# Two-layer transformer kernel: experts for all tokens against experts for the tokens that chose them

## The chip, the cores and the metric

The kernel runs on one core of a Trainium2 chip. The metric is the device time of one execution in microseconds (us). A core has TensorE (PE), VectorE (DVE), ScalarE (ACT), GpSimd (POOL) and SyncE (SP); each runs its own instruction list in order, and they wait for one another with semaphores. DMA transfers are issued here from SP and, after the change, from POOL too. PE writes into eight PSUM banks, which DVE and ACT read.

## What is computed

Two transformer layers on `x` of 4 batches x 512 tokens x 256 numbers. The first layer (softmax attention and a plain linear layer) and the second layer's linear attention with 16 heads stay as they are. The change is in the last part, the second layer's feed-forward with 8 experts of width 176, of which each token uses two, and one shared expert of the same width:

```python
logits = jnp.einsum('th,eh->te', x, gate_w)
scores = jax.nn.softmax(logits, axis=-1)
topk_w, topk_idx = lax.top_k(scores, 2)
topk_w = topk_w / (topk_w.sum(-1, keepdims=True) + 1e-20)
cw = jnp.zeros((T, 8)).at[jnp.arange(T)[:, None], topk_idx].add(topk_w)
def body(acc, ew):
    w1e, w2e, cwe = ew                  # 256 x 352 and 176 x 256
    g, u = jnp.split(x @ w1e, 2, axis=-1)
    return (acc + cwe[:, None] * (jax.nn.silu(g) * u @ w2e), None)
moe, _ = lax.scan(body, jnp.zeros_like(x), (w1, w2, cw.T))
shared = (silu(x @ sw1.T) * (x @ sw2.T)) @ sw3.T
```

The layer's output is `x + gb * (moe + shared)`. All of it is float32.

## The kernel before, in words

Three stages run one after the other, with a barrier between them: `front_stage`, `attention1_stage` and `experts_stage`. `x` (16 tiles of 128 tokens), the normalized tokens `h_parts` and the attention output `yacc` stay in SBUF.

A float32 product is made of three matmuls: both operands are split into a high part (a copy to the format fp32r by ACT) and a low part (a subtraction by DVE or POOL), and `TERMS` names the pairs high-high, high-low and low-high that are summed in PSUM.

**Attention stage.** The 16 heads go in 8 pairs (`over_pairs`: the first, a loop over six, the last; SP's own loop loads for the next pair). While one pair is worked on, SP loads the next pair's weights (L1152, 1 MB into `wraw`), which ACT splits at the end of the pair (L1295) and POOL completes (L1503). In the last pair `LateNorm` already normalizes batch 0 for the experts. At the stage's end SP loads the first weight tiles of the experts.

**Experts stage.** The hidden units of the 8 experts (8 x 176 = 1408, 11 tiles of 128) and of the shared expert (2 tiles) form 13 tiles. For each of 4 batches and each of 13 tiles PE makes gate and up (L1635: two times six matmuls of 512 tokens), ACT takes silu (L1772), DVE multiplies (L1886, L1893), ACT and DVE split the product (L1748, L1842), and PE multiplies it with the down weights into the output (L1647: twelve matmuls of 256 columns), one tile behind. Routing is a factor: a small matmul (L1718) spreads each token's eight weights over the hidden units, zero for six of the experts, and DVE multiplies with it (L1890). So each token passes through all experts. The routing weights of the next batch (logits L1659, the two largest scores, L1794 to L1821) and its norm (POOL's L968, L980, L983, L996, L998, ACT's L974, PE's L956, L1011) are made in between, at set tiles of the batch before (`ahead`). The weights arrive in the first batch: SP loads a tile (L1620), ACT copies the high part (L1733), POOL subtracts the low part (L1924). At each batch's end DVE applies the layer's gate (L1850), POOL adds to `x` (L1930), SP stores (L1623, and L1627 for the last batch).

The order on every queue is written out by hand; there is no planner.

## Time and profile before

| | us |
|---|---|
| median of three executions | 1311.54 (1310.83 to 1311.84) |
| the profiled execution, its own time | 1312.52 |
| its span, first to last instruction | 1310.8 |
| front stage | 0 to 311.7 |
| attention stage | 311.7 to 1050.4 |
| experts stage | 1050.4 to 1310.8 |

The profile is of one execution. Busy time leaves out register, semaphore and DMA-issuing instructions. Matmuls overlap, so the sum of their durations is more than the time they take together. PEclk is the clock granted to TensorE as a share of 2.4 GHz. "Idle before, releaser" is how long an engine stood before a group and which instruction ended it.

### The profile page before, as it was taken

The page shows a single profiled execution, that of the slowest core. Times are in us where ns is not written, and L with a number is a line of the kernel's source. Part 1 is how long each engine was busy: PE and PEld are TensorE (multiplying, and loading weights), DVE is VectorE, ACT ScalarE, POOL GpSimd, SP SyncE. Part 2 cuts the span into 40 slices and gives each one's busy share as a digit, 9 for nine tenths or more (in the row PEclk, how much of TensorE's full clock was granted, in tenths as well). Part 3 has the DMA queues.
Part 4 walks back from the last instruction along what each step waited for, and adds up shares of the span by engine and source line. Part 5 has one row for each costly group of instructions (what it writes and reads, how often), then busy time and mean ns, then how long its engine had stood idle before and what let it go on. Part 6 is the DMA issues. An engine that isn't in the chain of part 4 may idle for free. (4 is left out here: it accounts for less than half of the span.)

```text
span 1310.8 us, 21088 instructions
## 1 busy us (share of the span) xinstructions
PE 1174.9 (90%) x7620; PEld 992.9 (76%) x7620; DVE 917.2 (70%) x1619; ACT 727.7 (56%) x1315; POOL 350.7 (27%) x305
## 2 busy tenths in 40 slices
PE   5878787743999999999999999999999879999998
PEld 4545565533988988988989889889888758888886
DVE  4578888614777778787777777787788656565544
ACT  4568676623766665656566666656565434333322
POOL 6275453423112121121121121211213145202000
PEclk8689888956999999999999999999999889999999
DMA  7100001001001001000010010010000022000000
GB/s 279 50 29 5 17 3 49 1 1 56 9 1 49 10 9 40 8 16 32 8 48 8 2 46 8 8 40 8 17 25 1 0 84 61 18 0 17 1 17 17
DMA packets 16451, 35.94 MB, mean 27 GB/s; under 512 B 3330, under 2 KB 5634, under 8 KB 15363
## 3 DMA queue, kind: packets, MB, share of 16 engines
q1 hardware_dynamic: 16386, 35.09, 8.3%
q8 instruction: 40, 0.66, 0.2%
q14 instruction: 25, 0.20, 0.1%
HBM read 26.69 MB, written 6.29 MB: 25 GB/s over the span
## 5 line engine op out<-in xcount | busy, mean ns | idle before, releaser
L1194 PE MATMUL attn_psum<-all_h_parts,attn_wp 128*128 128x512 f32 x1152 | 304.2, 400 | 8.4 <-POOL attn_wp L1503 8.4
L1194 PEld LDWEIGHTS attn_psum<-all_h_parts,attn_wp 128*128 128x128 f32 x1152 | 213.8, 191 | 50.4 <-POOL attn_wp L1503 8.8
L1331 ACT CAST attn_pp<-attn_p 128x512 fp32r<-128x512 f32 (+3 forms) x256 | 117.2, 458 | 219.1 <-DVE attn_p L1412 219.0
L1393 DVE TENSOR_TENSOR attn_pp<-attn_p,attn_pp 128x512 fp32r<-128x512 f32 (+3 forms) x256 | 192.5, 752 | 2.3 <-ACT attn_pp L1331 2.3
L1513 POOL TENSOR_TENSOR all_gate<-all_gate,attn_sq 128x512 f32<-128x512 f32 x64 | 91.4, 1428 | 330.4 <-ACT attn_sq L1342 330.4
L1261 PE MATMUL attn_psum<-attn_qkp 128*128 128x512 f32 (+3 forms) x768 | 165.6, 325 | 4.1 <-DVE attn_qkp L1393 4.1
L1220 PE MATMUL attn_psum<-attn_pp,attn_vp 128*128 128x512 f32 (+3 forms) x768 | 163.0, 322 | 0.0
L1635 PE MATMUL experts_psum<-all_h_parts,experts_wf 128*128 128x512 f32 x624 | 156.4, 398 | 0.0
L1220 PEld LDWEIGHTS attn_psum<-attn_pp,attn_vp 128*128 128x128 f32 x768 | 130.0, 190 | 19.6
L1261 PEld LDWEIGHTS attn_psum<-attn_qkp 128*128 128x128 f32 x768 | 125.6, 190 | 12.9 <-issue 4.6
L1635 PEld LDWEIGHTS experts_psum<-all_h_parts,experts_wf 128*128 128x128 f32 x624 | 114.2, 189 | 24.5 <-DVE experts_wf L1874 0.5
L1393 DVE TENSOR_TENSOR attn_yp<-attn_y,attn_yp 128x512 fp32r<-128x512 f32 x64 | 67.3, 1052 | 92.3 <-ACT attn_yp L1339 92.3
L1412 DVE TENSOR_TENSOR attn_p<-attn_psum,attn_mask 128x512 f32<-128x512 f32 (+3 forms) x256 | 123.7, 483 | 5.3 <-PE attn_psum L1261 3.8
L757 DVE TENSOR_REDUCE front_top<-front_psum 128x2 f32<-128x256 f32 (+3 forms) x128 | 100.6, 816 | 34.2 <-PE front_psum L463 34.0
L1204 PE MATMUL attn_psum<-attn_wop,attn_yp 128*128 128x256 f32 x768 | 105.0, 288 | 17.2 <-DVE attn_yp L1393 17.2
L1204 PEld LDWEIGHTS attn_psum<-attn_wop,attn_yp 128*128 128x128 f32 x768 | 98.6, 197 | 19.0 <-DVE attn_yp L1393 19.0
L1189 PE MATMUL attn_psum<-attn_wp,all_h_parts 128*128 128x256 f32 x768 | 102.3, 282 | 1.1
L606 ACT ACTIVATE front_probs<-front_psum 128x1024 f16<-128x1024 f32 (+3 forms) x128 | 83.7, 705 | 33.5 <-PE front_psum L470 33.3
L1393 DVE TENSOR_TENSOR attn_qkp<-attn_qk,attn_qkp 128x512 fp32r<-128x512 f32 x128 | 88.8, 694 | 18.1 <-ACT attn_qkp L1306 18.1
L1189 PEld LDWEIGHTS attn_psum<-attn_wp,all_h_parts 128*128 128x128 f32 x768 | 95.0, 188 | 3.5 <-ACT attn_qk L1303 3.5
L1647 PE MATMUL experts_psum<-experts_wf,experts_hidp 128*128 128x256 f32 x624 | 91.2, 295 | 6.2 <-DVE experts_hidp L1842 6.2
L1647 PEld LDWEIGHTS experts_psum<-experts_wf,experts_hidp 128*128 128x128 f32 x624 | 82.4, 192 | 9.1 <-DVE experts_hidp L1842 7.2
(241 smaller groups left out, 1743.4 us busy)
## 6 DMA issues: line engine op xcount, KB each, us to landing
all_wraw<-in_w1p SPq DMA_DIRECT2D x8, 1024.0 KB, 4.8
all_wraw<-in_wf SPq DMA_DIRECT2D x13, 384.0 KB, 3.2
attn_mask<-decay_masks SPq DMA_DIRECT2D x16, 256.0 KB, 2.6
all_x<-in_x SPq DMA_DIRECT2D x4, 512.0 KB, 10.9
decay_masks<-all_wraw SPq DMA_DIRECT2D x8, 256.0 KB, 5.8
decay_masks<-all_yacc SPq DMA_DIRECT2D x8, 256.0 KB, 8.4
front_kt<-front_kall SPq DMA_DIRECT2D x64, 32.0 KB, 1.9
attn_woraw<-in_wout SPq DMA_DIRECT2D x8, 256.0 KB, 2.6
```

The lines of the kernel that those rows point to most:

```text
L757: nc.vector.tensor_reduce(top[:, tt, h:h + 2], banks(ev)[:, :, 0:(tt + 1) * P], AX.X, ALU.max).then_inc(top_done, 1)
L1189: last = nc.tensor.matmul(out[:, i * 2 * P:(i + 1) * 2 * P], hh[:, a, k, tt * P:(tt + 1) * P], wp[:, c, k, col:col + 2 * P], start=(m == 0 ...
L1194: last = nc.tensor.matmul(out, wp[:, a, k, col:col + P], hh[:, c, k, b * S:(b + 1) * S], start=(m == 0), stop=(m == 5))
L1204: last = nc.tensor.matmul(ps[:, Y_BANK + i, half * D:(half + 1) * D], yp[:, a, h, tt * P:(tt + 1) * P], wop[:, c, h, :], start=(m == 0), s ...
L1220: last = nc.tensor.matmul(ps[:, O_BANK + h, j * P:S], vp[:, b % 2, a, j, h * P:(h + 1) * P], pp[:, h, c, OFF[j]:OFF[j] + S - j * P], start ...
L1261: last = nc.tensor.matmul(bank(task)[:, 0:S - j * P], qkp[:, h, a, 1, j * P:(j + 1) * P], qkp[:, h, c, 0, j * P:S], start=(m3 == 0), stop= ...
L1331: nc.scalar.copy(pp[:, u % 2, 0, cols], p[:, cols]).then_inc(p_hi, 1)
L1393: nc.vector.tensor_tensor(out, whole, high.bitcast(F32), ALU.subtract).then_inc(ready, 1)
L1412: nc.vector.tensor_tensor(p[:, cols], bank(task)[:, 0:S - j * P], mask[:, u % 2, 0:S - j * P], ALU.mult).then_inc(p_masked, 1)
L1513: nc.gpsimd.tensor_tensor(cols, cols, sq[:, h, :], ALU.add).then_inc(summed, 1)
L1635: last = nc.tensor.matmul(ps[:, bank, :], wf[:, a, f, col:col + P], hh[:, c, k, b * S:(b + 1) * S], start=(m == 0), stop=(m == 5))
L1647: last = nc.tensor.matmul(y_out(b, tt), hidp[:, c % 2, a, tt * P:(tt + 1) * P], wf[:, w, EXPERT_ORDER[fi], 2 * KT * P:WF], start=(fi == 0 ...
```

## The change

The experts are computed only for the tokens that chose them. Two arrays in DRAM are new: `expert_rows` with a region of 2048 rows for each of the 8 experts, and `expert_results` with a row for each token's first and second choice, and spare rows behind them. A row (`ROW` = 258 numbers) holds the 256 normalized numbers of a token, its weight for this expert and the number of the result row it belongs to.

In the attention stage SP fills the regions: zeros over 257 numbers of each row, one region at a time, and one integer a row that points to a spare result row.

In the experts stage PE works only on the two shared tiles of each batch (`FS` = 2). Beside them `Router` finds for each token its two experts and its rank among the tokens of each (a matmul with a triangle of ones and with ones), and from them a row number (`slot`). PE turns the tokens back to rows (`token_rows`), ACT copies them twice into `rows_out`, and POOL sends them with indirect DMAs, eight a batch, each of 128 rows, to the regions. After the last batch `vector_map` works out which expert and which 128 rows each of `TILES` = 39 tiles has; 39 is the most that 4096 rows in 8 regions can fill. `block_i` holds the block numbers, `packed_i` eight expert numbers in one integer. The weights of the 8 experts (`wx`, 1216 numbers a partition each) are loaded and split beside the batches, the low parts of four by POOL and of four by DVE.

Then the 39 tiles go through a pipeline of four steps: rows turned (`turn`), gate and up (`hidden_of`: six matmuls of 352 columns, weights at an address from a register), the product turned (`turn_hidden`), down (`down_of`: six of 256 columns); ACT scales the result with the token's weight, and POOL sends it with an indirect DMA to `expert_results`. The rows lie in a ring of `RING1` = 4 places. At the end SP loads both results of each token, DVE adds them and applies the gate, POOL adds to `x`, SP stores.

The first lines are of the attention stage (`sp`); lines taken out are given as "..." here.

```diff
+                sp.wait_ge(empty_set, 2)
+                zeros = empty[:, :].unsqueeze(1).to_broadcast([P, B * TB, ROW - 1])
+                ends = no_token[:, :].rearrange("p (e i) -> p e i", e=E)
+                region = t["rows_dram"].rearrange("(e i p) n -> e p i n", e=E, p=P)
+                sp.dma_start(region[E - 1, :, :, 0:ROW - 1], zeros).then_inc(emptied_rows, 16)
+                with nc.allow_non_contiguous_dma(reason="one number per row"):
+                    for e in range(E):
+                        sp.dma_start(region[e, :, :, ROW - 1:ROW].bitcast(I32), ends[:, e, :].unsqueeze(2)).then_inc(emptied_rows, 16)
                 with sp.Fori(0, PAIRS - 1) as it:
+                    sp.dma_start(region[bass.ds(it, 1), :, :, 0:ROW - 1].rearrange("a p i n -> (a p) i n"), zeros
+                                 ).then_inc(emptied_rows, 16)
                     sp.wait_ge(w_ready[2], it + 1)
                     sp.dma_start(wraw[:, :, :], d["w1p"][bass.ds(it + 1, 1)].rearrange("a p k n -> (a p) k n")
                                  ).then_inc(w_loaded, 16)
```

From the new class `Router`, rank and slots:

```diff
+            out = bank[:, RANK_AT + tt * E:RANK_AT + (tt + 1) * E]
+            nc.tensor.matmul(out, self.tri[:, :], self.any[:, b, tt, :], start=True, stop=(b == 0 and tt == 0))
+            earlier = [self.seen[:, before, :] for before in range(b)] + [self.any[:, b, before, :] for before in range(tt)]
+            for i, chosen in enumerate(earlier):
+                last = nc.tensor.matmul(out, self.ones[:, :], chosen, start=False, stop=(i == len(earlier) - 1))
+        last.then_inc(self.ranked, 1)
...
+        dve.wait_ge(self.ranked, b + 1)
+        nc.vector.tensor_tensor(self.rank[:, :, :], bank[:, RANK_AT:RANK_AT + TB * E].rearrange("p (t e) -> p t e", e=E),
+                                self.base[:, :].unsqueeze(1).to_broadcast([P, TB, E]), ALU.add).then_inc(self.rank_read, 1)
+        dve.wait_ge(self.rank_read, b + 1)
+        for c in range(2):
+            last = nc.vector.tensor_tensor(self.picked[:, c], self.chosen[:, c], self.rank[:, :, :], ALU.mult)
+        self.then(dve, last)
+        self.then(dve, nc.vector.tensor_reduce(self.slotf[:, :, :], self.picked[:, :, :, :], AX.X, ALU.add))
+        nc.vector.tensor_copy(self.slot[:, b], self.slotf[:, :, :]).then_inc(self.slot_done, 1)
```

SP's part of the experts stage (`xraw` holds the ring of rows once the weights are split):

```diff
+        rowt = xraw[:, 0:RING1 * ROW].rearrange("p (r n) -> p r n", r=RING1)
...
+                sp.wait_ge(route.map_done, 2)
+                sp.wait_ge(scattered, B * 2 * TB * 16)
+                for j in range(TILES):
+                    r = j % RING1
+                    if j >= RING1:
+                        sp.wait_ge(turned, j - RING1 + 1)
+                        sp.wait_ge(y_scaled, j - RING1 + 1)
+                        sp.wait_ge(y_sent[r], j // RING1 * 16)
+                    at_block = sp.value_load(route.block_i[0:1, j:j + 1], min_val=0, max_val=E * B * TB - 1)
+                    sp.dma_start(rowt[:, r, :], rows_dram[bass.ds(at_block, 1)].rearrange("a p n -> (a p) n")
+                                 ).then_inc(row_full[r], 16)
+                for r in range(RING1):
+                    sp.wait_ge(y_sent[r], len(range(r, TILES, RING1)) * 16)
+                for b in range(B):
+                    for c, (to, loaded) in enumerate(((first_y[:, rows(b), :], first_in), (second_y[b], second_in))):
+                        sp.dma_start(to, t["y_dram"][c * B * S + b * S:c * B * S + (b + 1) * S].rearrange(
+                            "(t p) n -> p t n", p=P)).then_inc(loaded[b], 16)
+                for b in range(B):
+                    sp.wait_ge(x_final, b + 1)
+                    sp.dma_start(t["out"][:, rows(b), :], x[:, rows(b), :]).then_inc(stored, 16)
+                sp.wait_ge(stored, 16 * B)
 
```

PE's (`token_rows` once a batch, the rest for each of the 39 tiles):

```diff
+                def token_rows(b):
+                    if b == 0:
+                        pe.wait_ge(ident_ready, 1)
+                    for half in range(2):
+                        if b or half:
+                            pe.wait_ge(rows_read, 2 * (2 * b + half))
+                        for i in range(2):
+                            tt = b * TB + half * 2 + i
+                            for k in range(KT):
+                                for a in range(2):
+                                    last = nc.tensor.matmul(ps[:, R_BANK, i * D + k * P:i * D + (k + 1) * P],
+                                                            hh[:, a, k, tt * P:(tt + 1) * P], identr[:, :],
+                                                            start=(a == 0), stop=(a == 1))
+                        last.then_inc(rows_made, 1)
...
+                def turn(j):
+                    pe.wait_ge(row_full[j % RING1], (j // RING1 + 1) * 16)
+                    if j >= 2:
+                        pe.wait_ge(t_low, j - 1)
+                    for k in range(KT):
+                        last = nc.tensor.transpose(ps[:, j % 2, k * P:(k + 1) * P], rowt[:, j % RING1, k * P:(k + 1) * P],
+                                                   t["ident"][:, :])
+                    last.then_inc(turned, 1)
+
+                def expert_of(j):
+                    if j % E == 0:
+                        experts.append(pe.value_load(route.packed_i[0:1, j // E:j // E + 1], min_val=0, max_val=E ** E - 1))
+                    return pe.snap((experts[-1] // E ** (j % E)) % E, min_val=0, max_val=E - 1)
+
...
+                def down_of(j, e):
+                    pe.wait_ge(ht_low, j + 1)
+                    if j >= 2:
+                        pe.wait_ge(y_scaled, j - 1)
+                    for m, (i, (a, c)) in enumerate([(i, tc) for i in range(2) for tc in TERMS]):
+                        col = KT * 2 * I + i * D
+                        last = nc.tensor.matmul(ps[:, 6 + j % 2, 0:D], turned_hidden(j, a)[:, i, :],
+                                                wx[0:IH, c, bass.ds(e, 1), col:col + D].rearrange("p e n -> p (e n)"),
+                                                start=(m == 0), stop=(m == 5))
+                    last.then_inc(y_made, 1)
+
...
+                for s in range(TILES + 3):
+                    if s < TILES:
+                        turn(s)
+                    if 1 <= s < TILES + 1:
+                        at_expert[s - 1] = expert_of(s - 1)
+                        hidden_of(s - 1, at_expert[s - 1])
+                    if 2 <= s < TILES + 2:
+                        turn_hidden(s - 2)
+                    if s >= 3:
+                        down_of(s - 3, at_expert.pop(s - 3))
 
```

ACT's copies and, of its loop over the tiles, the first and the last part:

```diff
+                def take_rows(b):
+                    for half in range(2):
+                        act.wait_ge(rows_made, 2 * b + half + 1)
+                        if b and half == 0:
+                            act.wait_ge(scattered, b * 2 * TB * 16)
+                        for c in range(2):
+                            nc.scalar.copy(rows_out[:, c, 2 * half:2 * half + 2, 0:D],
+                                           bank(R_BANK).rearrange("p (t n) -> p t n", t=2)).then_inc(rows_read, 1)
+
...
+                for s in range(TILES + 3):
+                    j = s
+                    if j < TILES:
+                        act.wait_ge(turned, j + 1)
+                        if j == 0:
+                            act.wait_ge(down_done, FS * B)
+                        if j >= 2:
+                            act.wait_ge(h_made, j - 1)
+                        nc.scalar.copy(turned_rows(j, 0), bank(j % 2)[:, 0:D].rearrange("p (k n) -> p k n", k=KT)
+                                       ).then_inc(t_high, 1)
+                    j = s - 1
+                    if 0 <= j < TILES:
...
+                    j = s - 3
+                    if j >= 0:
+                        act.wait_ge(y_made, j + 1)
+                        if j >= RING1:
+                            act.wait_ge(y_sent[j % RING1], j // RING1 * 16)
+                        elif j == 0:
+                            act.wait_ge(x_added, B)
+                        nc.scalar.activation(upd[:, j % RING1, :], ps[:, 6 + j % 2, 0:D], ACT.Identity,
+                                             scale=rowt[:, j % RING1, D:D + 1]).then_inc(y_scaled, 1)
```

The first of DVE's three parts for a tile and its end, and POOL's order:

```diff
+                for s in range(TILES + 2):
+                    j = s
+                    if j < TILES:
+                        dve.wait_ge(t_high, j + 1)
+                        nc.vector.tensor_tensor(turned_rows(j, 1), bank(j % 2)[:, 0:D].rearrange("p (k n) -> p k n", k=KT),
+                                                turned_rows(j, 0).bitcast(F32), ALU.subtract).then_inc(t_low, 1)
...
+                for b in range(B):
+                    dve.wait_ge(first_in[b], 16)
+                    dve.wait_ge(second_in[b], 16)
+                    y = first_y[:, rows(b), :]
+                    nc.vector.tensor_tensor(y, y, second_y[b], ALU.add).then_inc(y_sum, 1)
+                    dve.wait_ge(y_sum, b + 1)
+                    nc.vector.tensor_tensor(y, y, t["gate"][:, 3, b:b + 1, :].to_broadcast([P, TB, D]), ALU.mult
+                                            ).then_inc(y_gated, 1)
...
+                def scatter(b):
+                    pool.wait_ge(route.slot_done, b + 1)
+                    pool.wait_ge(meta_set, b + 1)
+                    pool.wait_ge(rows_read, 4 * (b + 1))
+                    for tt in range(TB):
+                        for c in range(2):
+                            nc.gpsimd.indirect_dma_start(
+                                t["rows_dram"], bass.IndirectOffsetOnAxis(ap=route.slot[:, b, c, tt:tt + 1], axis=0),
+                                rows_out[:, c, tt, :], None).then_inc(scattered, 16)
+
+                route.pool_tables(nc, pool)
+                for b in range(1, B):
+                    norm.pool_rms(nc, pool, b - 1, b)
+                norm.pool_update(nc, pool, 0, 1)
+                norm.pool_update(nc, pool, 1, 2)
+                norm.pool_rstd(nc, pool, 0)
+                w_lower(0)
+                norm.pool_update(nc, pool, 2, 3)
+                route.pool_map_tables(nc, pool)
+                norm.pool_rstd(nc, pool, 1)
+                scatter(0)
+                w_lower(1)
+                norm.pool_rstd(nc, pool, 2)
+                w_lower(2)
+                scatter(1)
+                w_lower(3)
+                scatter(2)
+                scatter(3)
+
+                for j in range(TILES):
+                    r = j % RING1
+                    pool.wait_ge(y_scaled, j + 1)
+                    pool.wait_ge(row_full[r], (j // RING1 + 1) * 16)
+                    nc.gpsimd.indirect_dma_start(
+                        t["y_dram"], bass.IndirectOffsetOnAxis(ap=rowt[:, r, D + 1:D + 2].bitcast(I32), axis=0),
+                        upd[:, r, :], None).then_inc(y_sent[r], 16)
```

## Rows read from the trace of the kernel before

**Rows 1.** The page, part 1: busy us (share) x instructions, by engine:

```profile
PE 1174.9 (90%) x7620; PEld 992.9 (76%) x7620; DVE 917.2 (70%) x1619; ACT 727.7 (56%) x1315; POOL 350.7 (27%) x305
```

**Rows 2.** Windows of the last stage: busy us of each engine, PEclk, DMA share, GB/s:

```profile
1050.40:1310.80 260.40, 249.16 (x1396) 203.65 (x1396) 142.54 (x307) 87.22 (x147) 55.88 (x32) 0.98 0.09 27
```

**Rows 3.** The chain that ended last: start us, us, engine, line, instructions:

```profile
1111.20 1.63 PE experts_psum L1647 x12
...
1112.84 2.81 PE experts_psum L1635 x12
```

**Rows 4.** Groups by line and shape, POOL: busy us, mean ns | idle before:

```profile
L1924 POOL TENSOR_TENSOR experts_wf<-all_wraw,experts_wf 128x768 fp32r<-128x768 f32 x12 | 22.5, 1882 | 28.0 <-ACT experts_wf L1733 27.9
...
L983 POOL TENSOR_TENSOR all_x<-all_x,all_yacc 128x1024 f32<-128x1024 f32 x4 | 10.9, 2720 | 0.3
...
L980 POOL TENSOR_TENSOR all_yacc<-all_yacc,all_gate 128x1024 f32<-128x1024 f32 x4 | 9.6, 2404 | 12.8 <-ACT all_yacc L974 12.8
...
L998 POOL TENSOR_TENSOR experts_n_rstd<-experts_n_rstd,all_neg_half 128x4 f32<-128x4 f32 x3 | 3.1, 1040 | 0.3
...
L996 POOL TENSOR_SCALAR experts_n_rstd<-experts_n_mv 128x4 f32<-128x4 f32 x3 | 1.7, 577 | 13.6 <-DVE experts_n_mv L991 13.6
```

**Rows 5.** SP's own instructions for the mask loads (ns min/median/max):

```profile
L1160 SPq MOVE attn_mask<-decay_masks x14: 29/29/29, 393.7 to 946.0; - x14
...
L1160 SPq DMA_DIRECT2D attn_mask<-decay_masks x14: 332/333/333, 393.8 to 946.1; - x14
```

**Rows 6.** The page, part 6: DMA issues, KB each, median us from issue to landing:

```profile
all_wraw<-in_w1p SPq DMA_DIRECT2D x8, 1024.0 KB, 4.8
...
attn_mask<-decay_masks SPq DMA_DIRECT2D x16, 256.0 KB, 2.6
...
out<-all_x SPq DMA_DIRECT2D x3, 512.0 KB, 2.6
...
out<-all_x SPq DMA_DIRECT2D x2, 256.0 KB, 2.0
...
attn_normw<-in_norm_w SPq DMA_DIRECT2D x1, 8.0 KB, 1.5
```

**Rows 7.** Groups by line and shape, ACT and DVE:

```profile
L1748 ACT CAST experts_hidp<-experts_hid 128x512 fp32r<-128x512 f32 x52 | 32.2, 620 | 91.8 <-DVE experts_hid L1890 78.0 <-DVE experts_hid L1893 13.8
...
L974 ACT ACTIVATE all_yacc<-all_yacc,all_rms 128x256 f32<-128x256 f32 x16 | 6.8, 499 | 0.0
...
L1850 DVE TENSOR_TENSOR experts_upd<-experts_psum,all_gate 128x1024 f32<-128x1024 f32 x3 | 3.6, 1214 | 0.0
```

**Rows 8.** Timeline, first batch of the last stage, POOL and DVE: start us, us:

```profile
1057.98 3.59 POOL L1924 TENSOR_TENSOR experts_wf<-all_wraw,experts_wf 128x768 fp32r<-128x768 f32 x2 [2.15 <-ACT experts_wf L1733]
...
1058.09 3.53 DVE L1814 TENSOR_TENSOR experts_chosen<-experts_expert_id,experts_best_idf 128x32 f32<-128x32 f32 x2
```

**Rows 9.** A window of low clock, and timeline of PE at either level:

```profile
262.00:300.00 38.00, 13.75 (x80) 11.37 (x80) 8.55 (x19) 9.05 (x14) 10.49 (x9) 0.54 0.00 1
...
211.77 1.06 PE L200 MATMUL front_psum<-all_ident,all_yacc 128*128 128x128 f32 x8 [0.63 <-ACT all_yacc L192]
...
304.55 1.94 PE L200 MATMUL front_psum<-all_ident,all_yacc 128*128 128x128 f32 x8 [9.77 <-ACT all_yacc L192]
...
314.87 4.82 PE L1194 MATMUL attn_psum<-all_h_parts,attn_wp 128*128 128x512 f32 x12 [8.38 <-POOL attn_wp L1503]
```

**Rows 10.** Timeline of the last store:

```profile
1306.37 0.69 DVE L1914 TENSOR_TENSOR all_x<-all_x,experts_upd 128x512 f32<-128x512 f32 x1
...
1307.08 1.66 SPq L1627 DMA_DIRECT2D out<-all_x  x2
```

**Rows 11.** Weights of the second pair (timeline); packets of queue 1 (page, part 3):

```profile
318.57 0.36 SPq L1152 DMA_DIRECT2D all_wraw<-in_w1p  x1
...
386.64 1.29 POOL L1503 TENSOR_TENSOR attn_wp<-all_wraw,attn_wp 128x512 fp32r<-128x512 f32 x1 [8.98 <-ACT attn_wp L1295]
...
q1 hardware_dynamic: 16386, 35.09, 8.3%
```

736 lines of the change are left out of this document (420 added, 316 removed).

## The prediction

> **What bounds the kernel now.** I read the busy shares first, then the window of the last stage, then the chain that ended last. TensorE (PE) is busy in 90% of the span [rows 1]; the stage that changes most is the last one, from 1050.4 to 1310.8 us, and there PE is busy in 249.2 of 260.4 us at a granted clock of 0.98, while the DMA engines have 9% to do [rows 2]. The chain through this stage is nearly PE alone: twelve matmuls of 512 columns in 2.81 us, twelve of 256 in 1.63 us [rows 3], 52 times (4 batches by 13 tiles), some 231 us of the 260. So the stage is bound by arithmetic, and every token goes through all eight experts though it needs two. Removing three quarters of that work is worth having only if what orders the rest is no slower.
>
> **What goes.** 44 of the 52 tiles go, each 2.81 + 1.63 us on the chain [rows 3]: 195 us. The eight of the shared expert stay.
>
> **What comes, part one: routing and scatter.** The order of POOL's instructions decides it. POOL's own work: three updates of 2.40 + 2.72 (15.4), three roots of 0.58 + 1.04 (4.9), three of 1.04 for the mean square (3.1), four low halves of weights, 1.88 x 1216/768 = 2.98 each (11.9) [rows 4], and ten small operations for tables, at 0.4 each (the smallest arithmetic here is 0.58) 4 us: 39 us. Then 32 indirect scatters. The trace has no such issue. From below it costs what SP needs to issue a DMA, 0.33 [rows 5]; from above the 1.88 of POOL's pass over 768 columns [rows 4], rounded to 2.0, since it must go through 128 indices. I take 1.0, nearest to POOL's smallest costly operation (1.04 on four columns, [rows 4]): 32 us. The scatters of batches 1, 2 and 3 also wait each for the landing of the batch before (2.0, as a store of 256 KB, [rows 6]) and four copies of 0.62 on ACT [rows 7] (2.4), since `rows_out` is single: 13 us. About 8 us more are waited for the first norm and the last ranks. Sum 92 us, of which PE's shared tiles (8 x 4.4 = 36 us), its turns and ranks, ACT's splits and the weights' loads lie beside POOL. Bounds: 32 scatters at 0.33 and no waits for first norm and last ranks, 63; at 2.0, 124. POOL and DVE can also hold each other up: two small compares took 3.53 us while POOL's low halves ran [rows 8]; a few us, inside these bounds.
>
> **Part two: 39 tiles, and a ring of four.** This is the term that decides. PE at step j does turn(j), hidden(j-1), turn_hidden(j-2), down(j-3). SP may load rows j only after `turned`, `y_scaled` and `y_sent` of tile j-4. But down(j-4) is the last thing PE does in step j-1, and turn(j) the first in step j. So between two steps stands a whole round trip that nothing covers, and it is paid by each of tiles 4 to 38, 35 times:
> - PE's step. 512 columns cost 2.81/12 = 234 ns and 256 cost 136, so 352 cost about 172. Six of those 1.03, six of 256 0.82, four fp32 transposes about 0.13 each (eight took 1.06, [rows 9]) 0.5: 2.4 us with the last one's drain. At the lower clock more: the same eight transposes took 1.94 and twelve of 512 columns 4.82 instead of 2.81 [rows 3, 9], factors 1.83 and 1.72. 4.2 us.
> - ACT scales the result: 0.5 [rows 7].
> - POOL issues the indirect store: 1.0 (0.33 to 2.0, as above).
> - The store of 128 KB lands: 2.0 (1.5, an 8 KB load, to 2.6, a 512 KB store, [rows 6]).
> - SP loads the block number from SBUF into a register. The trace shows a register move, 0.03 [rows 5], and as far upper bound a whole memory trip of 1.5 [rows 6]; I take 0.7, in the middle, since neither is near.
> - SP issues the load, 0.33 [rows 5]; 129 KB land in 2.2, between 1.5 for 8 KB and 2.6 for 256 KB [rows 6].
> - Five handovers, 0.3 in all; SP issued 0.02 us after the result it waited for in the trace's last store [rows 10], so 0.1 from below and 0.5 from above.
>
> Chosen sum: 4.2 + 0.5 + 1.0 + 2.0 + 0.7 + 0.33 + 2.2 + 0.3 = 11.2 us a tile. Lowest 6.7 (PE 2.4), highest 14.2. DVE's three passes, ACT's other three and PE's register arithmetic for the expert number fit under the trip. 35 x 11.2 = 392; before it the first load and four steps, 15; behind it three steps and the last store, 14: 421 us.
>
> **The clock.** Before the second stage PE was busy for 13.75 of 38 us and was granted 0.54, that is mostly the lower level (1.2 GHz) [rows 9]. A tile with 4.2 busy of 11.2 is busier by no more than a little (38% to 36%), so I take the lower level. The Trainium skill says against this change, in "TensorE: Matmul & The Clock Gate", section "HAM oscillation", that a kernel which waits for a DMA in each tile is throttled again in each; by that rule PE's step is 4.2, without it 2.4, and the total some 70 us less. The trace agrees as far as it goes.
>
> The Trainium skill's page "DMA: Bandwidth & Descriptors", section "Anatomy of one DMA", fits a DMA issued from GpSimd by about 2.0 us plus bytes over 436e3 per us, all told. For 128 KB that is 2.3 us where I have 3.0 for issue and landing; by it the total would be about 27 us lower (35 tiles and the three waits of the scatters). No indirect DMA is in this trace.
>
> **Part three: the end.** Eight loads of 512 KB; 1 MB lands in 4.8 [rows 6], so the fourth pair at about 18; then DVE 2 x 1.2 [rows 7], POOL's addition 2.7 [rows 4], the store 2.6 [rows 6]: 26 us (20 to 30).
>
> **Part four: in the attention stage** SP also queues zeros (2.1 MB eight times) and 16384 numbers of 4 bytes, ahead of the second pair's weights. Those are issued at 318.6 now and used only at about 386 [rows 11]: 67 us of cover. I cost this at nothing. If the cover is gone: queue 1 took 8.3% of 16 engines for 16386 packets [rows 11], 0.106 us each; 1024 numbers and 256 zero rows per engine at that price are 136 us, and PE would stand for some 64. But the mean packet carries 2.1 KB and these 4 bytes.
>
> **The sum.** 1050.4 + 92 + 421 + 26 = 1589 us of span, plus 1.7 outside it (the profiled execution is 1312.5 for a span of 1310.8): 1591. That execution is 1.0 above the median of 1311.5, so 1590. The three runs lie within 0.08%; I call 0.2% what can be told from no change. Break-even: 260.4 - 92 - 29 - 26 (fill and drain of part two are the 29) leaves 113 us for 35 tiles, 3.2 us each; the two landings alone are 3.0 at their lowest.
>
> **Rivals.**
> - *A cheaper trip*, 8.5 us: transfers, issue and register load at their low ends with the clock low, or 9.4 with the clock high and the rest as chosen. For it: the small transfers of this trace are quick. From 1590 that takes 35 x 2.7 and 21 us of scatters, or 35 x 1.8: 1474 to 1527 us. Both together (6.7 us, 1411) have next to nothing. Chance 0.22.
> - *A dearer trip*, 12.5 to 14.2 us: POOL works out 128 addresses slowly, both landings 2.6. Nothing in the trace excludes it, as no scatter to DRAM is in it. 35 x 1.3 more is 1636, 35 x 3.0 and 32 us of scatters 1727. Chance 0.13.
> - *The 4-byte numbers hold up the second pair's weights*: + 64, 1655. Chance 0.07.
> - *Faster*: the ring doesn't bind. Its place is SP's wait before loading rows j; it decides if rows of tile j are in SBUF when PE ends step j-1, and the change breaks even where a step with its trip is 3.2 us. Then PE's 39 steps at the full clock are all: 39 x 2.5 + 15 = 113, and 1050.4 + 92 + 113 + 26 + 1.7 = 1283 us. For it: PE's work does fall to a third. Against it: the wait is on the landing of the result of the very tile PE has just finished. Chance 0.03.
>
> **The numbers.** The forecast (trip of 10 to 12.5 us, 1548 to 1636) has 0.55. The range 1470 to 1715 takes in the cheap rival, the numbers' delay and the nearer part of the dear one. Slower 0.96, within 0.2% 0.01, faster 0.03.
>
> **What would show it.** The timeline of the last stage: turns of PE some 11 us apart from the fifth tile on, PE's idle time there ended by the load of rows, SP's by the indirect stores (or named by ACT's scaling before them), PE busy under half at a granted clock near 0.5; the first row load some 92 us after the stage starts, POOL the engine before it. Wrong: turns 2.5 to 4 us apart; a first phase above 125 us; a gap on PE near 386 us.

## The result, and the profile after the change

| | before | after |
|---|---|---|
| median of 4 runs, us | 1311.69 | 1607.24 |
| lowest to highest | 1310.83 to 1312.17 | 1606.55 to 1607.79 |
| ratio | | 1.2254, interval [1.2233, 1.2275] |
| profiled execution (its span) | 1312.5 (1310.8) | 1607.8 (1606.0) |
| TensorE (PE) busy | 1174.9 us, 90% | 1159.8 us, 72% |

The kernel became slower by 22.5%, 17 us beyond the forecast of 1590. The page of the kernel after, parts 1 and 4 (the second row is the chain that ended last, shares of the span by engine):

```profile
PE 1159.8 (72%) x7260; PEld 992.5 (62%) x7260; DVE 911.9 (57%) x1647; ACT 743.5 (46%) x1397; POOL 415.3 (26%) x379
...
issue 22%; POOL 3%; PE 1%; DMA 1%; POOLq 0%; ACT 0%; DVE 0%; SPq 0%; ACTq 0%
```

Against [rows 1], PE lost only 15 us of work, though 44 of 52 tiles are gone: the new tiles and transposes are nearly as many instructions (7260 against 7620), narrower ones, and they run partly at the lower clock. The chain has 22% under "issue", time in which the profile sees no wait. In the loop this is one piece of about 9 us for each tile, from the end of one indirect store's issue to the start of the next; it holds the landing of the store, the next load and PE's step, which the chain does not tell apart. The windows show where the time lies (us; busy time of PE, PEld, DVE, ACT, POOL with instructions; granted clock; DMA share; GB/s). The cuts are the start of the last stage, the first load of rows, the first load of results and the end:

```profile
0.00:1050.90 1050.90, 923.30 (x6224) 787.03 (x6224) 779.20 (x1312) 640.20 (x1168) 295.35 (x276) 0.94 0.17 44
1050.90:1198.60 147.70, 78.93 (x412) 64.97 (x412) 71.33 (x210) 44.10 (x73) 71.30 (x61) 0.70 0.19 63
1198.60:1575.90 377.30, 157.57 (x624) 140.50 (x624) 45.99 (x117) 59.24 (x156) 37.52 (x39) 0.67 0.09 28
1575.90:1606.00 30.10, 0.00 (x0) 0.00 (x0) 15.40 (x8) 0.00 (x0) 11.18 (x4) 0.50 0.60 209
```

Where [rows 2] had one stretch of 260 us with PE busy in 96% of it, there are now three, 147.7 + 377.3 + 30.1 us, with PE busy for 53%, 42% and nothing. All before the last stage is as it was: it starts at 1050.9 (1050.4 before).

**One tile of the loop**, timeline of the kernel after (start us, us, engine, line, instructions; in brackets the idle time before them and what ended it):

```profile
1308.02 0.69 PE L1935 MATMUL experts_psum<-all_ident,experts_xraw 128*128 128x128 f32 x2 [6.01 <-DMA experts_xraw<-expert_rows]
...
1308.36 2.11 PE L1949 MATMUL experts_psum<-experts_wx,all_h_parts 128*128 x6
...
1310.27 0.63 PE L1959 MATMUL experts_psum<-all_ident,all_gate 128*88 128x128 f32 x2
...
1310.55 1.63 PE L1969 MATMUL experts_psum<-experts_wx,all_h_parts 88*128 x6
...
1312.21 0.47 ACT L2084 ACTIVATE all_gate<-experts_psum,experts_xraw 128x256 f32<-128x256 f32 x1 [0.91 <-PE experts_psum L1969]
1312.96 0.96 POOL L2240 DMA_INDIRECT expert_results<-all_gate,experts_xraw  x1 [9.21 <-ACT all_gate L2084]
1316.12 0.33 SPq L1840 DMA_DIRECT2D experts_xraw<-expert_rows  x1
...
1318.29 0.69 PE L1935 MATMUL experts_psum<-all_ident,experts_xraw 128*128 128x128 f32 x2 [6.11 <-DMA experts_xraw<-expert_rows]
```

Read it from top to bottom as one circle: PE's step takes 4.2 us (1308.02 to 1312.2), then PE stands until the next turn 6.1 us later. The period is 1318.29 - 1308.02 = 10.27 us. The waits name both halves of the circle, first PE's for the rows (1198.6 to 1576 us), then SP's for the result of four tiles before (1190 to 1600 us):

```profile
PE experts_psum L1935 <- DMA experts_xraw<-expert_rows: 226.5, 37, 14.1
```

```profile
SPq L1838 <- DMA expert_results<-all_gate,experts_xraw: 319.7, 35, 10.2
```

Two more views of the same kernel give the parts of the trip that the timeline leaves out, the landings (median us from issue, for twelve tiles) and what SP does to get the block number into a register (ns min/median/max):

```profile
experts_xraw<-expert_rows SPq DMA_DIRECT2D x12, 129.0 KB, 2.0
expert_results<-all_gate,experts_xraw POOLq DMA_INDIRECT x12, 2.4
```

```profile
L1839 SPq TENSOR_LOAD <-experts_block_i x39: 263/267/478, 1197.6 to 1561.2; - x39
L1839 SPq FUSED_REGOPS  x39: 152/152/183, 1198.1 to 1561.5; - x39
```

**The first phase.** The waits of all engines from 1050 to 1200 us, longest sums first (sum, times, longest):

```profile
DVE experts_rank L1702 <- PE experts_psum L1695: 39.5, 4, 11.6
POOL experts_n_rstd L1003 <- DVE experts_n_mv L998: 32.3, 3, 16.1
POOL expert_rows L2213 <- DVE experts_slot L1709: 31.6, 2, 16.6
...
PE experts_psum L1896 <- ACT experts_rows_out L2016: 25.3, 4, 12.6
```

Nobody is the bound here: PE is busy for 79 us of 148, POOL and VectorE (DVE) for 71 each. DVE waits for ranks, POOL for slots, PE for the copies of rows, and each for another. The experiments had to say which of these waits are links of a chain and which are slack.

### The profile page after: what moved, and what is told of

Same layout as the page of the kernel before. It is cut to its first block and busy times, and to the rows that moved or that the text cites. A ratio compares the mean times of both kernels' runs of the same rounds, so it can differ in the third digit from the quotient of the medians.

```text
span 1606.0 us, 21440 instructions
## 1 busy us (share of the span) xinstructions
PE 1159.8 (72%) x7260; PEld 992.5 (62%) x7260; DVE 911.9 (57%) x1647; ACT 743.5 (46%) x1397; POOL 415.3 (26%) x379
## 5 line engine op out<-in xcount | busy, mean ns | idle before, releaser
L1935 PE MATMUL experts_psum<-all_ident,experts_xraw 128*128 128x128 f32 x78 | 26.5, 443 | 226.5 <-DMA experts_xraw<-expert_rows 226.5
L2176 DVE TENSOR_TENSOR all_h_parts<-experts_psum,all_h_parts 128x256 fp32r<-128x256 f32 x39 | 16.6, 424 | 270.9 <-ACT all_h_parts L2060 270.7
L1935 PEld LDWEIGHTS experts_psum<-all_ident,experts_xraw 128*128 128x128 f32 x78 | 11.4, 203 | 236.4 <-DMA experts_xraw<-expert_rows 222.2
L2240 POOL DMA_INDIRECT expert_results<-all_gate,experts_xraw x39 | 37.5, 962 | 340.8 <-ACT all_gate L2084 340.5
L2060 ACT CAST all_h_parts<-experts_psum 128x256 fp32r<-128x256 f32 x39 | 14.5, 372 | 239.6 <-PE experts_psum L1935 239.4
```

The lines of the kernel that those rows point to most:

```text
L2240: nc.gpsimd.indirect_dma_start(t["y_dram"], bass.IndirectOffsetOnAxis(ap=rowt[:, r, D + 1:D + 2].bitcast(I32), axis=0), upd[:, r, :], None ...
```

## The experiments

Two questions: what sets the period of a tile, and what makes the first phase 148 us long where I had 92. The table gives every kernel's time (median where it was timed in rounds, else one execution) and the lengths of the three stretches in its profile.

| kernel | us | first phase | tiles | end |
|---|---|---|---|---|
| after | 1607.2 | 147.7 | 377.3 | 30.1 |
| e1_ring5 | 1425.0 | 146.9 | 195.3 | 30.1 |
| e10_ring6 | 1359.1 | 141.5 | 134.9 | 30.1 |
| e2_ring8 | 1324.5 | 149.3 | 92.3 | 30.2 |
| e3_warm | 1566.7 | 146.0 | 338.0 | 30.1 |
| e4_late | 1596.5 | 136.3 | 377.4 | 30.1 |
| e5_meta | 1588.4 | 126.8 | 378.8 | 30.2 |
| e6_rank | 1577.2 | 115.7 | 378.6 | 30.2 |
| e11_double | 1647.1 | 184.0 | 377.7 | 32.8 |
| e7_ring8late | 1311.4 | 138.0 | 92.9 | 30.2 |
| e8_ring8all | 1289.4 | 112.4 | 92.5 | 30.1 |
| e9_first | 1289.4 | 114.3 | 92.4 | 30.1 |

Only e7, e8 and e9 were timed in rounds; the other eight are single executions. The kernel before took 1310.4 to 1311.7 us beside them (medians), its single executions 1307.9 to 1313.2. The first phase of one and the same code came out between 141.5 and 149.3 us (after, e1, e2, e3, e10), so only differences well above that spread, or repeated ones, say anything about it.

### Five, six and eight places for rows

```diff
-        rowt = xraw[:, 0:RING1 * ROW].rearrange("p (r n) -> p r n", r=RING1)
+        def rowt(j):
+            r = j % ROWS1
+            return xraw[:, r * ROW:(r + 1) * ROW] if r < 4 else raw[:, (r - 4) * ROW:(r - 3) * ROW]
...
-                    if j >= RING1:
-                        sp.wait_ge(turned, j - RING1 + 1)
-                        sp.wait_ge(y_scaled, j - RING1 + 1)
-                        sp.wait_ge(y_sent[r], j // RING1 * 16)
+                    if j >= ROWS1:
+                        sp.wait_ge(turned, j - ROWS1 + 1)
+                        sp.wait_ge(y_scaled, j - ROWS1 + 1)
+                        sp.wait_ge(y_sent[(j - ROWS1) % RING1], ((j - ROWS1) // RING1 + 1) * 16)
```

Only the buffers for rows grow (`ROWS1` is 5, 6 or 8); those for results stay four. SP also waits for the last expert's weights before its first load, since the new places lie in their raw buffer.

> The changed kernel with five places for rows instead of four; the fifth lies in the upper buffer of the raw weights. Theory (a round trip between two steps): in the changed kernel's trace turns of PE are 10.27 us apart, 4.0 of it PE's step and 6.3 the trip; with n places the trip is shared by n-3 steps, so (4.0 + 6.3) / 2 = 5.1 us a tile and about 1430 us in all. Rival (the tile is limited by something inside the step, DVE, ACT or register work of PE that the waits only hide): the period stays above 7 us, total above 1490.

> Eight places for rows. Theory: the trip is fully covered and PE's step is all; PE is then busy nearly all the time and its clock goes up, so 2.5 to 3.0 us a tile, total 1607 - 35 x 7.5 = about 1345. If the clock stays low: 4.0 a tile, about 1390. Rival (indirect stores on POOL or the DMA queues bind next): a tile needs POOL's 0.96 + 0.3 at least, so they could bind only below 1.3 us; a period above 4 us would mean a further wait that neither trace shows.

> The change with six places for rows. Theory (a tile's turn waits for a store R - 3 turns back, so the period is TensorE's step and the trip of 6.2 us over R - 3, or TensorE's step if that is longer): (2.4 + 6.2) / 3 = 2.9 us at the high clock, up to 3.4 us if the clock is low again in part (4.2 + 6.2 over 3), against 2.12 us with eight places; 1324.5 + 37 x 0.8 = 1354 us, up to 1372. Rival (the gain from five to eight places came from something else, such as the queue's order): a period of 4 us or more, over 1385 us.

A stretch in the middle of the loop, windows of e1_ring5, e10_ring6 and e2_ring8:

```profile
1215.00:1375.00 160.00, 99.88 (x511) 92.14 (x512) 36.67 (x95) 45.78 (x127) 29.82 (x31) 0.81 0.16 51
```

```profile
1220.00:1300.00 80.00, 65.34 (x376) 61.22 (x377) 26.81 (x70) 32.93 (x93) 21.91 (x23) 0.83 0.25 79
```

```profile
1220.00:1280.00 60.00, 60.00 (x456) 58.88 (x455) 31.84 (x85) 37.56 (x115) 27.61 (x29) 1.00 0.41 127
```

A tile has 16 matmuls, so the windows hold 31.9, 23.5 and 28.5 tiles: periods of 5.01, 3.40 and 2.11 us, beside 10.27 with four places. Times R - 3 the first three are 10.3, 10.0 and 10.2: **one round of about 10.2 us carries R - 3 tiles**, until PE's own step is longer than that share. That is so with eight places: PE is busy for 60.00 of 60.00 us at full clock, and the loop is bound by arithmetic at last. I had expected 2.5 to 3.0 us a tile and about 1345 us in all; it was 2.11 and 1324.5. All of the 285 us that the loop lost against eight places went with one wait, paid once per tile: the wait itself, and the low clock that came with it (next experiment). In the last row PE never stands for the expert number in a register, and the indirect stores at 0.96 us lie beside PE.

With six places I had 2.9 us at the high clock and 3.4 with the clock low in part; it is 3.4. The timeline shows three tiles in 10.26 us, the first of them still at the low clock:

```profile
1230.13 0.44 PE L1939 MATMUL experts_psum<-all_ident,experts_xraw 128*128 128x128 f32 x2 [1.83 <-DMA experts_xraw<-expert_rows]
1230.43 1.71 PE L1953 MATMUL experts_psum<-experts_wx,all_h_parts 128*128 x6
...
1237.45 0.95 PE L1973 MATMUL experts_psum<-experts_wx,all_h_parts 88*128 x6
1240.39 0.44 PE L1939 MATMUL experts_psum<-all_ident,experts_xraw 128*128 128x128 f32 x2 [1.99 <-DMA experts_xraw<-expert_rows]
```

### Keeping PE busy while it waits

```diff
                     if s >= 3:
                         down_of(s - 3, at_expert.pop(s - 3))
+                    if 3 <= s < TILES - 1:
+                        for _ in range(90):
+                            nc.tensor.matmul(ps[:, 2 + s % 2, 0:P], route.ones[:, :], route.tri[:, :], start=True, stop=True)
```

Ninety matmuls of 128 columns whose result nobody reads fill most of the trip; the ring stays at four.

> Ring of four as in the changed kernel; after each tile's step PE makes 90 more matmuls of 128 columns into a PSUM bank that nobody reads then (no result changes). Theory (PE's step of 4.0 us is long because the clock is at its lower level while PE stands in the trip): PE stays busy, the granted clock goes to nearly 1.0, the 90 take about 5 us and fit into the trip of 6.3, and the step falls from 4.0 to 2.4: 8.7 us a tile, total about 1607 - 35 x 1.6 = 1550. Rival (the step is long for another reason, such as addresses from registers): the period stays at 10.3 or grows, total 1607 or more.

1566.7 us: 41 us less, with 3150 more matmuls (35 x 90), where I had expected 57 less. Window of the loop and the timeline of one tile, e3_warm:

```profile
1215.00:1500.00 285.00, 243.76 (x3285) 231.18 (x3284) 34.76 (x92) 45.12 (x124) 29.70 (x31) 0.96 0.10 30
```

```profile
1280.02 0.44 PE L1935 MATMUL experts_psum<-all_ident,experts_xraw 128*128 128x128 f32 x2 [1.06 <-DMA experts_xraw<-expert_rows]
1280.33 1.23 PE L1949 MATMUL experts_psum<-experts_wx,all_h_parts 128*128 x6
...
1281.53 0.96 PE L1969 MATMUL experts_psum<-experts_wx,all_h_parts 88*128 x6
1282.33 5.20 PE L1990 MATMUL experts_psum<-experts_tri,experts_ones 128*128 128x128 bf16 x90
...
1288.68 0.44 PE L1935 MATMUL experts_psum<-all_ident,experts_xraw 128*128 128x128 f32 x2 [1.15 <-DMA experts_xraw<-expert_rows]
```

Here a step takes 2.4 us and the period is 8.66: the trip is still 6.2 us. So the clock is worth 10.27 - 8.66 = 1.6 us in a tile that keeps it. The mean period of the window is 9.2 us (3285 matmuls at 106 a tile are 31 tiles in 285 us), because many tiles still fell to the low level: at 1308.42 the six matmuls of L1969 took 1.63 us again, not 0.96, and that tile's period was 11.0. The Trainium skill, "TensorE: Matmul & The Clock Gate", section "HAM oscillation", says that a kernel which stops for a DMA in each tile is throttled again in each, and this kernel's windows agree: 0.67 with the stops, 0.96 with the stops filled, 1.00 without stops. The 0.67 is a mean over two levels, as windows of one tile in the kernel after show:

```profile
1308.00:1312.20 4.20, 4.16 (x16) 3.73 (x16) 1.19 (x3) 1.06 (x3) 0.00 (x0) 0.50 0.01 2
1312.20:1315.20 3.00, 0.00 (x0) 0.00 (x0) 0.00 (x0) 0.47 (x1) 0.96 (x1) 1.00 0.11 44
1315.20:1318.20 3.00, 0.00 (x0) 0.00 (x0) 0.00 (x0) 0.00 (x0) 0.00 (x0) 0.56 0.17 44
```

PE does the whole step at 0.50; the clock is up (1.00) only in the idle time after it, when nothing uses it, and down again before the next turn. But the clock is the smaller part; the trip is the larger one.

### Where the first phase's time lies

**Weights split late** (e4_late): all eight low halves on DVE, none on POOL, and ScalarE (ACT) splits a batch's two experts after its rows are copied.

```diff
-POOL_LOWS = 4
+POOL_LOWS = 0
...
                     route.scalar_logits(nc, act, b, bank(ROUTE_BANK), logits_t)
-                    split(2 * b)
                     silu(2 * b)
...
                     high(2 * b + 1)
+                    if b == B - 1:
+                        take_rows(B - 1)
+                    split(2 * b)
                     split(2 * b + 1)
```

> Ring of four. In the batches' phase ACT splits the two expert weights of a batch only at the batch's end, behind the shared tiles and the rows, and DVE makes all eight low halves there (POOL none). Theory (the 148 us of this phase, where 92 were forecast, come from a circle through the queues: POOL's or DVE's low half, SP's next load, ACT's split ahead of silu and of the rows): the first load of rows comes 25 us or more earlier, total 1575 to 1585. Rival (the phase is set by POOL's order and the single rows_out alone, as in the forecast's sum): only POOL's 11 us of low halves can go, and less of it where POOL waits anyway: total 1597 to 1607.

1596.5 us, 11 less: the rival's case (half a us below its range), and with eight places the same edit took 11 us out of the first phase again (149.3 to 138.0). The handover of raw weights was not the circle I had looked for. What this trace does show is a wait that has grown (7.1 us in the kernel after), beside one of the longest old ones:

```profile
PE experts_psum L1896 <- ACT experts_rows_out L2016: 33.6, 4, 12.9
...
DVE experts_rows_out L2129 <- DMA expert_rows<-experts_rows_out,experts_slot: 16.5, 3, 6.6
```

L2129 is `meta`: DVE writes a batch's places and weights into `rows_out`. This waits for the landing of the batch before, and behind it on DVE stands `hide` of the shared expert, on which ACT, PE and so the next ranks and slots depend. That gave two edits, one on top of the other:

```diff
                     lower(c)
-                    meta(b)
                     hide(c + 1)
                     lower(c + 1)
...
                     if b + 1 < B:
                         norm.vector_low(nc, dve, b, b + 1)
+                        if b:
+                            meta(b)
                     output(b)
```

> e4_late with one more edit: VectorE writes a batch's numbers into rows_out (meta) after the batch's slots and the norm's low part, no longer between the two parts of the shared expert. Theory (one buffer rows_out closes a circle from the landing of a batch's rows through VectorE to the next batch's slots): in e4_late VectorE stood 6.61, 5.29 and 4.59 us before meta on the landing of the batch before, 16.5 us together, with the whole chain to the next slots behind it, so first row load at about 1172 us (1187.2 in e4_late) and 1582 us in all (1578 to 1588). ScalarE's copies into rows_out still wait for the same landing, so a part of it may return there: 1588 to 1592 if so. Rival (the first phase is bound by the norms and the shared expert, not by this wait): 1594 to 1599.

```diff
+                    route.tensor_rank(nc, pe, b, bank(ROUTE_BANK))
                     token_rows(b)
                     down(b * FS)
-                    route.tensor_rank(nc, pe, b, bank(ROUTE_BANK))
                     down(b * FS + 1)
```

> e5_meta with one more edit: on TensorE the ranks of a batch come before its token rows and not after them and the first down product. Theory (ranks, and so slots, were late only because they stood behind the rows' copies, 12 to 13 us of waiting on TensorE, and 2.9 us of down product): slots are ready when the rows are, and a batch's period falls to 8 scatters of 1.27 us, a landing of 2.5 us and four copies of rows with TensorE's second half (about 5.5 us), 18 to 20 us against about 28: first row load at about 1155 us, 1566 us in all (1560 to 1572). Rival (the rows' copies or the norm end last, not the slots): within 3 us of e5_meta.

(The first batch's `meta` stays in place; the last batch's comes after its slots.) 1588.4 and 1577.2 us: both gained, both less than the theory's main figure (1582 and 1566), e6_rank by more than its range allowed (up to 1572). The first phase fell by 9.5 and 11.1 us; each alone is little more than its spread of 7.8, the two together (20.6, and 25.6 from e7_ring8late to e8_ring8all) are well above it. Moving `meta` gave 8 us, the case in which part of the wait returns: POOL, which had waited for slots, now waited 24.7 us for `meta`. Moving the ranks gave another 11 where 16 were expected. The wait of POOL then names the copies of rows; the rows of e5_meta and of e6_rank:

```profile
POOL expert_rows L2212 <- DVE experts_rows_out L2130: 24.7, 2, 14.6
```

```profile
POOL expert_rows L2212 <- ACT experts_rows_out L2016: 26.3, 4, 10.8
```

The three edits together took 32 us out of the first phase. All its instructions are still there; only their order, and the engine of four low halves, changed.

**Twice the scatters** (e11_double), on the change itself:

```diff
-                        for c in range(2):
+                        for c, to in ((0, "rows_dram"), (1, "rows_dram"), (0, "rows_spare"), (1, "rows_spare")):
                             nc.gpsimd.indirect_dma_start(
-                                t["rows_dram"], ...
+                                t[to], ...
```

> The change with each scatter followed by its like: the same rows go a second time, to a tensor of their own that nobody reads, so each batch has 16 scatters. Theory (every batch's scatters lie in a circle: the landing frees rows_out, and the next slots come only behind what waits for it): 32 more scatters at 1.27 us all lie on the path, 1607 + 41 = 1648 us (1642 to 1654), first row load at about 1239 us. Rival (GpSimd's scatters run beside the norms and the shared expert, only the last batch's lie on the path): 8 x 1.27 = 10 us, 1615 to 1622. In between if the first phase has slack of its own.

1647.1 us, 40 more for 32 scatters of 0.96 us and their gaps of 0.30: 36 in the first phase, and nearly 3 in the end, for which I have no cause. Waits of e11_double:

```profile
PE experts_psum L1896 <- ACT experts_rows_out L2016: 56.0, 4, 24.5
...
DVE experts_rows_out L2128 <- DMA expert_spare<-experts_rows_out,experts_slot: 39.0, 3, 16.2
```

So every batch's scatters lie on the path, not the last one's alone: the price of the added ones came through `rows_out` (DVE's wait for the landing, 7.1 us in the kernel after, is 39.0 now, and PE's wait for the copies grew by 31). I forecast that POOL's scatters are on the path; this holds. What I missed is that much of the rest does not run beside them.

### All together

> e2_ring8 (eight places for rows) with the edit of e4_late. If what a tile costs and what the first phase costs are added end to end and do not share a resource: 1324.5 - 11.4 = 1313 us (1309 to 1317), a ratio to before of 1.002. Rival (with eight places the loop needs the weights of all experts at once, so that the later splits cost what they gave): 1320 to 1325.

e7_ring8late (eight places and late weights) took 1311.4 us against 1311.2, ratio 1.0004 [0.9993, 1.0015]: the two gains add up, 1324.5 - 11.4 = 1313.

> Eight places, late weights, meta and ranks moved: all edits together. By adding the terms, 1313 less what e6_rank gains on e4_late (about 30 us): 1283 us (1275 to 1292), faster than before by 2 per cent. If the first phase is bound elsewhere: 1308 to 1316, no difference from before.

e8_ring8all (also `meta` and the ranks) took 1289.4 against 1311.2, ratio 0.9837 [0.9818, 0.9856]: **faster than both kernels**, by 1.6% than the one before, which is small but clear of the interval. I had expected 1283, from a gain of 30 us by e6_rank on e4_late that turned out to be 19 (22 here, against e7_ring8late). Its windows:

```profile
1050.90:1163.30 112.40, 70.80 (x404) 58.64 (x403) 69.27 (x205) 42.86 (x71) 58.92 (x51) 0.75 0.24 82
1163.30:1255.80 92.50, 85.94 (x624) 82.93 (x624) 43.65 (x117) 52.12 (x156) 37.24 (x39) 0.94 0.36 113
1255.80:1285.90 30.10, 0.00 (x0) 0.00 (x0) 15.42 (x8) 0.00 (x0) 11.17 (x4) 0.50 0.59 209
```

**The first batch earlier** (e9_first): in e8_ring8all the first scatter starts at 1085.1 us, 34 us into the stage, behind a norm that has to be ready only for the next batch.

```diff
                     shared(b * FS + 1)
+                    if b == 0:
+                        pe.wait_ge(norm.mean_done, B - 1)
+                        route.tensor_rank(nc, pe, b, bank(ROUTE_BANK))
+                        token_rows(b)
...
-                norm.pool_rstd(nc, pool, 1)
                 scatter(0)
+                norm.pool_rstd(nc, pool, 1)
```

(with `take_rows(0)` and the first slots moved up in the same way)

> e8_ring8all with the first batch's rows sent earlier: its slots, ranks and token rows come before the next norm's turn on TensorE, VectorE and ScalarE, and its scatters before the second norm's root on GpSimd. In e8_ring8all the first scatter began 1085.1 us into the span, behind 12.5 us in which TensorE waited for the norm's VectorE part with the token rows queued behind it, and 5.6 us in which GpSimd waited for the second norm's statistics. Theory (the first phase is a circle of four batches through the one buffer rows_out, so what the first batch starts early the last one ends early): first scatter at about 1076 us, 1280 us in all (1277 to 1283). Rival (the batches after the first are bound by the norms, which this edit delays by the 10 us that GpSimd gives to scatters): 1287 to 1295, no gain or a loss.

1289.4 again, ratio to before 0.9834 [0.9816, 0.9852]: nothing gained. The first scatters of the four batches start at 1077.5, 1108.8, 1133.4 and 1152.3 us, in e8_ring8all at 1085.1, 1108.1, 1131.6 and 1150.4. The 7.6 us are won for the first batch and gone at the second. Just before it two waits stand in e9_first: POOL's for the norm, which its expectation's rival had named, and PE's for the shared expert, which it had not:

```profile
POOL experts_n_rstd L1004 <- DVE experts_n_mv L999: 12.5, 1, 12.5
```

```profile
1094.96 2.92 PE L1862 MATMUL experts_psum<-all_h_parts,experts_wsh 128*128 128x512 f32 x6 [5.92 <-DVE all_gate L2113]
```

So from the second batch on another chain is about as long as the circle through `rows_out`; by these two waits it goes through the norm and the shared expert. Which of its links is the longest I have not separated. A second `rows_out` was not tried.

## Why the prediction was right, and where its terms were not

The direction, the mechanism of the deciding term and the range held; that the sum came out only 1% low is luck: part one was 56 us too low, part two 44 us too high, and they stood against each other.

- **Part one, routing and scatter: this is the step that failed.** 92 us forecast, upper bound 124, measured 147.7. Among the prediction's own signs of being wrong stood "a first phase above 125 us", and it came. POOL's own work was right: 71.3 busy less 33.3 in scatters is 38.0, against 39. The 32 scatters are 0.96 us with 0.30 between them, 42 us against 32. The waits were the error: 67.5 us of POOL idle (147.7 - 71.3 - 8.9) against 13 + 8. I had let PE's tiles, turns and ranks "lie beside POOL" and had counted only the waits that `rows_out` makes on POOL's side. But `rows_out` is also waited for by DVE (`meta`) and ACT (`take_rows`), in whose queues the next batch's slots stand, so much of the work does not lie beside the scatters, it alternates with them: the first scatters of the four batches start at 1094.6, 1130.8, 1158.5 and 1185.9 us, the first 44 us into the stage and the others 27 to 36 us apart, with about 10 us of scatters in each. e11_double shows the scatters on the path; e5_meta and e6_rank that about 20 us of the rest were only order; e4_late that 11 us were in the splits, in POOL's share of them or in their place on ACT, which it does not separate. What is left in e6_rank, 115.7, is still 24 us above the forecast, though POOL no longer makes the 12 us of low halves that were in it. Of these 36 us, 16 are the dearer scatters (40.0 us busy there, 8.5 between them, against 32); what makes the other 20 stays open.
- **Part two, the ring of four: right.** 10.27 us a tile against 11.2, PE's idle time ended by the load of rows (226.5 us in 37 waits), PE busy in 42% of the loop. The parts, forecast and measured: PE's step 4.2 and 4.2; ACT 0.5 and 0.47; POOL's issue and landing 3.0 and 2.4; register load 0.7 and 0.7, from the store's landing at 1315.4 to SP's issue at 1316.12 (the two rows above are 0.42 of it); SP's issue and the landing of rows 2.5 and 2.2, from 1316.12 to 1318.29; the rest, handovers, 0.3 and 0.3. The issue on POOL (0.96 against 1.0) was right, but it lies inside the 2.4 us to the landing; I had added it. The fill and drain took 377.3 - 35 x 10.27 = 18 us, not 29. Together 44 us less than forecast, which is what hid part one's error.
- **The DMA rule.** The indirect store of 128 rows landed 2.4 us after its issue. The Trainium skill, "DMA: Bandwidth & Descriptors", section "Anatomy of one DMA", has a fit for a GpSimd DMA by which an estimate for this size is 2.3 us for the whole. That is nearer to the trace than the 3.0 in my sum, although the page does not say that the fit holds for indirect stores.
- **The clock: right where PE works.** A granted clock near 0.5 was forecast; the loop's mean is 0.67, but the step of 4.2 us is at 0.50, and the high level falls into PE's idle time. e3_warm gives the price, 1.6 us a tile, where I had 1.8.
- **Part three:** 30.1 against 26, at its upper bound of 30. Up to the landing of the last store it went as forecast: that store is issued at 1599.93, 24.0 us after the first load, where 18 + 2.4 + 2.7 is 23.1, and it lands in 2.6 [rows 6]. Then 3.3 us go by at the barrier that closes the stage, which I had left out (waits of SP in the last 26 us of the kernel after):

```profile
SPq L1820 <- PEq L1820: 3.3, 1, 3.3
SPq L1820 <- DMA out<-all_x: 2.3, 1, 2.3
```

- **Part four: right, nothing.** SP needed 25.7 us to issue the eight DMAs of 4-byte numbers, so the second pair's weights are issued at 343.30 and not 318.57, and behind the zeros they land in 14.2 us and not 5.2. ACT's first copy of them starts at 386.23, where it was at 385.95: from issue to use there are now 42.9 us and not 67.4, still more than the landing takes. POOL's operation on them starts at 386.92 where it was at 386.64 [rows 11], after the same wait of 8.97 us for ACT. (The rival's 64 us was mis-added: 136 less the 67 of cover is 69.)
- **The rivals.** Of the cheaper and the dearer trip the cheaper was the nearer: 10.27 lies between 9.4 and 11.2. But its 9.4 rested on a high clock, and what was cheaper here was the store's issue and landing. The rival "faster, the ring doesn't bind" is what e2_ring8 builds, and it had the loop right (92.3 us for the tiles, fill and drain with them, against 113), but the time was 1324.5 and not 1283, because the first phase ate the gain. With the measured terms the point from which the change pays is (260.4 - 147.7 - 18 - 30.1) / 35 = 1.8 us a tile, not 3.2; even a loop bound by PE at 2.11 us does not reach it until the first phase is reordered.

## What to carry to other kernels

Where a loop's buffer is freed by a transfer of the result, count how many steps lie between the last use and the next fill: with R places and results sent three steps late, one round trip carries only R - 3 tiles, and one more place can be worth more than everything else in the loop. And before work is called "beside" an engine's queue, follow every engine that waits for the same single buffer: what stands behind those waits in their queues is part of the path, and its order alone was worth about 20 us here, without a single instruction less.

## What the runs showed of the hardware that I had not expected

- An indirect DMA of 128 rows costs GpSimd 0.96 us, with 0.30 us to the next, and lands 2.4 us after its issue, where a plain load of that size lands in 2.0. Single ones took up to 3.65 us where DVE had large operations at the same time, in e8_ring8all beside two subtractions of 128x1216, which kept their 1.42 us each:

```profile
1090.91 3.65 POOL L2216 DMA_INDIRECT expert_rows<-experts_rows_out,experts_slot  x1 [0.31 <-issue]
```

  Elementwise operations of the two engines that overlap can stretch too, in the same kernel:

```profile
1069.45 2.35 POOL L988 TENSOR_TENSOR all_yacc<-all_yacc,all_gate 128x1024 f32<-128x1024 f32 x1
1069.65 2.70 DVE L2110 TENSOR_TENSOR experts_hidp<-all_gate,experts_hidp 128x512 fp32r<-128x512 f32 x1 [0.68 <-ACT experts_hidp L2012]
```

  The DVE operation takes 0.68 us otherwise. In the last 30 us of the kernel after, three of DVE's operations that overlapped POOL's additions took 2.96 to 3.25 us and the others 1.2; two of POOL's additions took 3.25 and the others 2.3.
- SyncE gets a number from SBUF into a register in 0.27 us, and issues the load that uses it about 0.7 us after it began (1315.4 to 1316.12); a matmul with the expert's address in a register runs as fast as PE can take it (60.00 of 60.00 us busy).
- 16384 writes of 4 bytes and 16 MB of zeros beside a busy stage cost next to nothing: the last stage starts at 1050.9 us where it started at 1050.4.
